# A small clear and a wait on GpSimd in front of every gather of gate rows, in a two-layer LSTM graph kernel

## What is computed

```python
def _lstm_last(seq, wih, whh, bih, bhh):      # seq: 33 steps x 512 nodes x 128
    def step(carry, x_t):
        h, c = carry
        g = x_t @ wih.T + h @ whh.T + b       # 512 x 512 gates
        i, f, gg, o = jnp.split(g, 4, axis=-1)
        c = sigmoid(f) * c + sigmoid(i) * tanh(gg)
        h = sigmoid(o) * tanh(c)
        return (h, c), None

def _sage_conv(x, src, ...):                  # run twice: conv1, relu, conv2
    msgs = x[src].reshape(n, d, c)
    aggr = _lstm_last(swapaxes(msgs, 0, 1), wih, whh, bih, bhh)
    return aggr @ wl.T + bl + x @ wr.T

x = layernorm(x + sage(sage(x)))
x = layernorm(x + relu(segment_sum((x @ weight[rel])[src] * norm, dst)))
```

## Time and profile before

| | |
|---|---|
| median of 3 runs | 535.96 us (535.65 to 536.25) |
| span of the profiled execution | 570.4 us |
| PE busy | 485.2 us (85%) |
| DVE busy | 399.5 us (70%) |
| ACT busy | 325.8 us (57%) |
| POOL busy | 309.4 us (54%) |
| mean granted TensorE clock | 0.963 |

### The profile page before, as it was taken

One profiled execution on the slowest core, in us unless ns is written; L12 is line 12 of the kernel. 1 busy time (PEld: TensorE's weight loads), 2 busy tenths in 40 slices (PEclk: granted clock), 3 DMA queues, 4 the chain that ended last, 5 costly groups with the idle time before them and its releaser, 6 DMA issues.

```text
span 570.4 us, 9783 instructions
## 1 busy us (share of the span) xinstructions
PE 485.2 (85%) x3463; PEld 349.4 (61%) x3463; DVE 399.5 (70%) x1114; ACT 325.8 (57%) x832; POOL 309.4 (54%) x320
## 2 busy tenths in 40 slices
PE   8766998979897999778897888887899987978795
PEld 4644786757676785656666766775785543444343
DVE  5544887858676895557776776876787975757665
ACT  4734766737556674545565665655675664545543
POOL 6476565665546501676664566666204655656551
PEclk9997999979999999978989999999999999999899
DMA  5665665675646502665665456556202111111111
GB/s 191 204 188 168 180 192 159 177 195 161 175 125 197 166 11 93 187 180 161 172 169 148 134 163 183 167 169 181 77 1 79 48 38 38 42 38 41 39 42 29
DMA packets 28346, 72.85 MB, mean 128 GB/s; under 512 B 6795, under 2 KB 10691, under 8 KB 28298
## 3 DMA queue, kind: packets, MB, share of 16 engines
q0 software_dynamic: 20768, 64.77, 40.0%
q1 hardware_dynamic: 6442, 6.54, 4.0%
q10 hardware_dynamic: 1088, 0.92, 0.5%
HBM read 69.05 MB, written 3.16 MB: 127 GB/s over the span
## 4 chain that ended last, share of the span: by engine, by line
PE 39%; DVE 17%; ACT 16%; another core or an unknown queue 13%; issue 8%; DMA 6%; POOL 1%; DVEq 0%; ACTq 0%; POOLq 0%
PE gates L1254 18%; DMA edge_rows<-msg_table,msg_index 6%; PE gates L1247 5%; PE work L1254 4%; DVE msg_full L1090 3%; ACT act_if L601 3%; ACT h_hi L597 3%; DVE prod_fc L906 2%; DVE prod_ig L908 2%; ACT msg_full L750 2%; PE work L1247 2%; DVE h_full L877 2%; ACT act_o L619 2%; ACT tanh_c L593 2%
## 5 line engine op out<-in xcount | busy, mean ns | idle before, releaser
L524 POOL DMA_INDIRECT rows<-gate_table,src_steps x226 | 224.7, 994 | 165.1 <-issue 64.5
L1247 PE MATMUL gates<-ident,rows 128*128 128x128 f32 x686 | 99.5, 281 | 39.5 <-issue 20.8
L601 ACT ACTIVATE act_if<-gates 128x512 f32<-128x512 f32 x113 | 67.8, 600 | 104.1 <-remote 54.5
L539 POOL DMA_INDIRECT edge_rows<-msg_table,msg_index x76 | 75.5, 993 | 79.6 <-DMA msg_table<-table_sb 30.9
L1254 PE MATMUL gates<-h_hi,whh_hi 128*128 128x256 f16 x396 | 104.7, 283 | 13.1 <-ACT h_hi L597 6.6
L906 DVE TENSOR_TENSOR prod_fc<-act_if,cell 128x256 f32<-128x256 f32 x128 | 54.2, 424 | 81.3 <-issue 37.3
L1247 PEld LDWEIGHTS gates<-ident,rows 128*128 128x128 f32 x686 | 78.1, 144 | 52.1 <-issue 49.7
L1254 PE MATMUL gates<-h_hi,whh_lo 128*128 128x256 f16 x396 | 104.1, 281 | 0.0
L1254 PE MATMUL gates<-h_lo,whh_hi 128*128 128x256 f16 x396 | 88.1, 282 | 0.4 <-issue 0.4
L890 DVE TENSOR_TENSOR h_lo<-h_full,h_hi 128x256 f16<-128x256 f32 x128 | 54.2, 423 | 12.3 <-ACT h_hi L597 0.9
L1080 DVE TENSOR_SCALAR rows<-node_iota,dst_f 128x512 f16<-128x512 f16 x132 | 43.4, 365 | 26.8 <-ACT msg_full L750 25.7
(11 more groups left out here) (186 smaller groups left out, 800.5 us busy)
## 6 DMA issues: line engine op xcount, KB each, us to landing
rows<-gate_table,src_steps POOLq DMA_INDIRECT x226
gate_table<-rows SPq DMA_DIRECT2D x8, 256.0 KB
edge_rows<-msg_table,msg_index POOLq DMA_INDIRECT x76
code<-code_table SPq DMA_DIRECT2D x6, 160.0 KB
msg_table<-table_sb SPq DMA_DIRECT2D x4, 192.0 KB, 2.4
code<-code_table SPq DMA_DIRECT2D x5, 128.0 KB
whhT<-turned_whh SPq DMA_DIRECT2D x2, 256.0 KB
wihT<-turned_wih ACTq DMA_DIRECT2D x1, 256.0 KB, 2.9
```

The lines of the kernel that those rows point to most:

```text
L524: pool.indirect_dma_start(rows[:, j * K + k, :], None, gate_table[l], bass.IndirectOffsetOnAxis(src_steps[:, t, k:k + 1], axis=0)).then_in ...
L539: pool.indirect_dma_start(edge_rows[:, c % 2, n, :], None, msg_rows, bass.IndirectOffsetOnAxis(msg_index[:, pool_first(c) + n:pool_first(c ...
L601: act.activation(act_if[:, h, :], gates[:, h, 0, :], ACT.Sigmoid, scale=1 / G_SCALE).then_inc(if_ready[h], 1)
L1247: pe.matmul(gate_place(t, h, gate)[:, k * P:(k + 1) * P], rows[:, j * K + 2 * h + k, gate * P:(gate + 1) * P], ident[:, :], is_transpose=True,
```

## The change

A tile `pause` of 128 x 256 float32 is added, and a semaphore `paused`. In front of each of the 226 gathers of gate rows, behind the waits that were there already, POOL clears the tile and then waits until the clear is complete; only then is the gather issued. Nothing else reads or writes the tile. The 8 gathers of L506 and the 76 gathers of the edge stage (L539) are as before.

```diff
+        pause = sb("pause", [P, 256], F32)
         stats = sb("stats", [P, K, 6], F32)
...
+        paused = sem("paused")
         iota_ready = sem("iota_ready")
...
                     if issued.index((turn, k)) >= UNDER_WAY:
                         landed, tile = issued[issued.index((turn, k)) - UNDER_WAY]
                         pool.wait_ge(rows_in[landed % DEEP * K + tile], 16 * rows_count(landed, tile))
+                    pool.memset(pause[:, :], 0.0).then_inc(paused, 1)
+                    pool.wait_ge(paused, issued.index((turn, k)) + 1)
                     pool.indirect_dma_start(
                         rows[:, j * K + k, :], None, gate_table[l],
                         bass.IndirectOffsetOnAxis(src_steps[:, t, k:k + 1], axis=0)
```

## The result

The changed kernel takes **568.54 us** in the median of 4 runs (565.9 to 573.8), the kernel before 535.81 us (535.04 to 536.25): a ratio of 1.0646 with a 95% interval of 1.0582 to 1.071, so 32.7 us slower. I had forecast slower, by 13 us. The direction was right and the time lies in the range, but the size was off by a factor of 2.5.

The account below looks back on a forecast made before the run. PE, DVE and ACT taking turns in the LSTM loop were taken as the bound, POOL beside them. A period of 1.65 us against 1.60 and 1.59 gave 5.4 + 6.8 us, rounded up to 13: 549 us, range 533 to 577.

Parts of the forecast that it names:

- the period that POOL can afford: Longest gather-to-gather time on POOL without delaying PE: 1.60 us in layer 0, 1.59 us in layer 1, for undisturbed runs.
- the last tiles are there about 10 us early: At step 32, gathered tiles land before PE's transposes need them: about 10 us in layer 0, 13 us in layer 1.
- I take the layers to shrink in proportion: Both layers scaled by 0.940, the median over the profiled execution (535.96 against 570.4 us), POOL's own instructions unscaled.
- The terms of the sum: POOL's new period: gather 0.99, clear 0.31, clear's end to gather 0.30, gather's end to clear 0.05; together 1.65 us.
- 81 us of added POOL time: 226 pauses of 0.36 us on POOL, claimed to be wholly absorbed in the profiled execution.
- 61 us of waits: POOL's waits before the change: 33.4 us for PE with the ring full, 27.8 us for landings; time held back.
- The port: SBUF port shared by POOL and DVE: clears charged nothing on DVE; effect on the sum under a microsecond.
- Hidden: Rival: POOL's period stays under what can be afforded in undisturbed runs too; time 536 us, chance 0.25.
- Much slower: Rival: 0.30 us stands behind each gather also before a clear; period 1.90 us, time 603 us, chance 0.09.
- Faster: Rival: gathers spread out stop disturbing the path, where ACT waits for an unnamed releaser; time 526 us, chance 0.14.
- The queue that I named behind the wait: Behind POOL's added wait: further gate-row gathers, then message gathers that wait 30.9 us for their table anyway; nothing lost.
- at most a few us in the profile: Sign: PE's waits, or ACT's without a named releaser, grow toward each layer's end, by at most a few us.

Follow-up runs that it names:

- run 1: The kernel before, with no edit, timed and profiled once more: 535.18 us, span of the profiled execution 533.5 us.
- run 5: The kernel before with the last tile's gather left out in all turns but the first five (174 gathers in place of 226): 486.33 us.
- run 12: The kernel before with six gathers under way in place of three (UNDER_WAY = 6), no pause: 483.89 us.
- run 9: The changed kernel with each clear waiting for the clear one gather earlier, and the gather not waiting for its own clear: 554.25 us.
- run 2: The changed kernel with a clear of 1 column in place of 256, the wait kept: 544.69 us.
- run 3: The changed kernel with a clear of 128 columns in place of 256, the wait kept: 557.77 us.
- run 4: The changed kernel with a clear of 512 columns in place of 256, the wait kept: 610.84 us.
- run 8: The changed kernel with four gathers under way in place of three (UNDER_WAY = 4): 558.8 us.

## Why the prediction was right and where it failed

**What bounds the kernel now: wrong.** The step that failed is the period that POOL can afford, 1.60 and 1.59 us, and behind it two premises: "the last tiles are there about 10 us early", and "I take the layers to shrink in proportion". I read a lead of 10 and 13 us, true of that one execution. In run 1 the last gather of layer 0 is used 3.6 us after its issue, which is the landing itself. The layers shrank by far more than in proportion: from 195 us each (14 to 209, 224 to 419) to 183 and 173 us in run 1. Those are 34 of the 36.9 us by which the spans differ, and 0.913 in place of 0.940. In the view by stretches of the trace before (columns as at the end of this document):

```profile
14.00:209.00 195.00, 164.83 (x1304) 130.84 (x1303) 137.08 (x379) 115.53 (x305) 111.75 (x112) 0.95 0.59 168
224.00:419.00 195.00, 164.94 (x1324) 132.28 (x1323) 139.78 (x376) 113.61 (x297) 112.72 (x114) 0.96 0.55 154
```

Had I taken the whole 34.4 us off the layers, the sum would have read (186.0 + 194.9 - 34.4 - 8) / 220 = 1.54 us, just the pace of run 1. I had the warning in hand, a profiled execution 6% longer than the median. There was a second one in the same trace: before the transposes PE stood idle for 21.4 us in 18 waits under "issue", the name under which its waits for tiles run in the changed kernel, the longest in the first steps of layer 0. I looked only at step 32, where there is none.

```profile
  issue: 21.4, 18
...
40.35 1.81 PE L1247 MATMUL gates<-ident,rows 128*128 128x128 f32 x6 [4.71 <-issue]
```

And the loop itself is quicker still: left alone it needs 484 to 486 us (runs 5 and 12), which is a pace of 1.30, not 1.60. In the kernel before the loop runs into the gathers and is held at 1.54.

Why that one execution was longer stays open. Its PE was busy 485.2 us against 465.7 in run 1 for the same 3463 instructions, at a mean granted clock of 0.963 against 0.979; that is 19.5 of the 36.9 us. The waits of ACT for an unnamed releaser are no separate loss: 54.5 + 47.6 = 102 us of waits of that line for it and for PE, against 96.6 us in run 1, all in PE's name there.

**The terms of the sum: three of four right.** Gather 0.99, measured 1.007. Clear 0.31, measured 0.327. Clear's end to gather 0.30, measured 0.27 in most rows and 66.6 / 226 = 0.29 in the mean. Gather's end to clear 0.05, measured 0.00. Sum 1.65, measured 1.63 in the mean where nothing else is waited for. The Trainium skill's statement (GPSIMD Engine Reference, Instruction dispatch) that completion holds back only what waits for it put the last term near its lower end and was nearer there than my 0.05; the trace agrees with it at 0.00 us between a gather and the clear behind it. The wait that I left out is the landing wait, which still comes on top: 11.5 us over 226 gathers, 0.05 us.

**What absorbs it: a real effect, in the wrong place.** I set 81 us of added POOL time against 61 us of waits and the lead, and found it all absorbed in the profile. (The 61 us also held 38 preparations of 0.30, 11 us, which stand ahead of a gather with or without a pause.) By the rows, from run 1 to the changed kernel: clears +74.0 us; gathers +1.6; POOL's idle time on both, 140.4 to 66.6 + 28.5, -45.3. The sum is +30.3 us, beside 32.7 in the time. Of the -45.3, the waits for landings without the preparation make 43 to 11.5, some -32, and the full ring (6.8 us with 9 preparations in it) -4. So POOL was the path for most of the time, and it was mainly the landing waits that paid for part of the pause. The stretches of the layers went from 183 and 173 us to 192 us each: layer 1, which had run ahead in its first half, lost twice as much as layer 0.

**The sum itself.** With what the runs show it would read: four terms, 1.63; landing waits, 0.05; against 1.54, not 1.60: (1.68 - 1.54) x 226 = 32 us. My 13 us came from differences of 0.05 and 0.06 us to an affordable period of 1.60 and 1.59. The mis-sized term is that period, too long by 0.05 to 0.06. That direction and range held owes something to luck: the mechanism that I gave, a lead used up in the last third of each layer, is not what the rows show, and the layers' new period was nearly right.

**The port: right.** DVE's operation for `h_lo` has 404 to 492 ns with a median of 425 in the changed kernel, against 405, 426 and 453 in the earlier trace rows, and DVE's whole busy time is 401.1 us against 398.5 in run 1. Nor do the clears slow the transfers: the median from issue to landing is 3.4 us in the changed kernel and 3.7 in run 1. The harm is on PE's side: PE, and behind it ACT and DVE, wait for tiles. PE's idle time ahead of the transposes is 66.3 us against 41.8 in run 1.

**The rivals.** Hidden fell by the size of the harm. Much slower (a gap of 0.30 behind the gather) fell: the gap is 0.00. Faster: the gathers did not disturb the path by being too dense. It is the opposite: with more under way the kernel is quicker by up to 50 us. The queue that I named behind the wait, the message gathers, lost nothing: they still wait 19.5 us for their table (18.2 in run 1).

**What I said would show it.** The clear 226 times with a mean of 0.31 (0.327), gathers 1.6 to 1.7 us apart (1.58 and 1.63 above), POOL's waits for PE gone: seen. Gathers of step 32 issued within 5 us of their use: seen (202.65 and 206.10 in layer 0). But "at most a few us in the profile" for PE's waits was wrong: they start in the first steps of layer 0, as those of run 1 do.

## What to carry to other kernels

When the profiled execution is longer than the median, slack read from it isn't slack: first find a row that tells who waits for whom in an execution as long as the median, or take the whole difference off the loop that the slack is measured against, not its share (here that gives 1.54 in place of 1.60). Count a wait only beyond what the instruction needs in any case. Ask of a rule that limits transfers under way whether it sets the pace; here one number, 3 to 6, was worth 9.3%. An engine whose queue is on the path pays for every instruction put into it, except for as much as it waited anyway.

## What I had not expected of the hardware

- More gathers under way hardly take longer each. The stretches of the two layers, run 12 and then run 1 (busy us of each engine, then clock, DMA share, GB/s):

```profile
14.00:165.00 151.00, 148.38 (x1311) 129.47 (x1308) 137.19 (x382) 114.72 (x307) 110.98 (x112) 1.00 0.74 218
179.00:331.00 152.00, 150.39 (x1331) 130.99 (x1329) 138.31 (x378) 112.68 (x300) 112.04 (x114) 1.00 0.70 198
```

```profile
14.00:197.00 183.00, 156.12 (x1313) 133.79 (x1312) 139.13 (x383) 114.92 (x306) 111.66 (x112) 0.98 0.63 180
210.00:383.00 173.00, 156.06 (x1327) 133.47 (x1326) 139.22 (x379) 113.56 (x300) 114.27 (x114) 0.98 0.63 174
```

  With six gathers of 256 KB under way they moved 218 and 198 GB/s, against 180 and 174 with three, and the median time from issue to landing, in the page's list of DMA issues, went only from 3.7 to 3.8 us. So the DMA engines had room. An estimate of what the limit does, from the rows: with three under way a gather at its own spacing of 1.29 us holds up the third behind it if its landing takes longer than 3 x 1.29 - 0.30 = 3.6 us, and the median is 3.7; with four the bound is 4.9 us, with six 7.4. The longest wait for a landing was 3.3 us with three, 2.2 with four and 1.1 with six. Why some landings take much longer than the median no run shows.
- POOL starts a clear in the very instant in which a gather ends (351.37 + 0.98 = 352.35), and a wait for an instruction of POOL itself costs about 0.10 us (0.27 against 0.17 in run 9).
- A gather was a little longer in some of the kernels with clears: mean 1.031, 1.028, 1.029 and 1.033 us in runs 2, 3, 4 and 9, against 1.000 in run 1, but only 1.007 in the changed kernel and 1.009 in run 8. I don't know why.
